# Four x tiles loaded ahead of the context's weights and split before them, and the second batch's matrix split in four parts

## The chip, the cores and the metric

The kernel runs on one core of one Trainium2 chip. The metric is the device time of one execution in microseconds (us), lower is better. Engine names are those of the profile: PE is TensorE's matmul side (PEld its weight loads), DVE is VectorE, ACT is ScalarE, POOL is GpSimd, SP is SyncE, which only issues transfers here.

## What is computed

Two batches of 2048 rows of 512 values pass through one decoder layer in f32: a self attention without softmax, a cross attention over 154 context rows with a mask, and a feed-forward step with a time shift, each followed by a layer norm.

```
attn = jnp.einsum('bhik,bhjk->bhij', q, k)          # self attention: no softmax, 8 heads of 64
out = jnp.einsum('bhik,bhkj->bhij', attn, v)        # so (q k^T) v = q (k^T v)
x = _layernorm(x + out @ w_o.T + b_o)
...
scores = jnp.einsum('bhqd,bhkd->bhqk', q, k) / jnp.sqrt(jnp.float32(D_K))   # 16 heads of 32, 154 keys
scores = jnp.where(Mask == 0, jnp.float32(NEG_INF), scores)
x = _layernorm(x + (softmax(scores) @ v) @ W_o.T + b_o)
...
xr = mu_r * x + (1.0 - mu_r) * x_prev ; xk = mu_k * x + (1.0 - mu_k) * x_prev
r = sigmoid(xr @ W_r.T) ; k_act = square(relu(xk @ W_k.T))
x = _layernorm(x + r * (k_act @ W_v.T))
```

Since the self attention has no softmax, it is one 512x512 matrix per batch, made from the sum of x^T x over the batch's rows. Each product that must keep f32's accuracy is made in three passes: both operands are split into a high part (a rounded copy, by ACT) and a low part (the difference, by DVE or POOL), and three of the four products are summed.

## The kernel before

There are two blocks with a barrier between them, each with one program written out by hand per engine. An engine runs its own list strictly in order; semaphores tie the lists together.

**The first block** (`prologue`) reads x in 32 tiles of 128 rows, 16 to a batch, through a ring of four buffers (`RING`). For tile j, SP loads it (`load(j)`, L183) once tile j-4 has been split and added; ACT makes the high part and its half (`high(j)`, L214 and L215); DVE adds the tile to a running column sum (L296) and makes the low part (`low(j)`, L300); PE adds the tile's products to four accumulator banks (`sums(j)`, L438 and L443). From tile 4 on `high(j)` waits until PE is done with tile j-4. Between these tiles stand the context's values and keys: ctx (616 KB), the value weights `cross_wv` and the key weights `cross_wk` (1 MB each) are loaded by SP, split by `part_high(i)` on ACT (L239) and `part_low(i)` on DVE (L330), i being 0 for ctx, 1 for cross_wv and 2 for cross_wk. PE multiplies them (three row tiles of values, then four column tiles of keys, L87 to L89), DVE takes the values with their bias (`v_raw`, L342), and ACT takes the keys (`kt`, L255). PE's list in the first block begins: tiles 0 to 5, values, keys, tiles 6 to 17. Later parts of the block fold the first batch's self attention into a matrix m.

**The second block** (`layers`) walks over 16 groups of 256 rows, 8 to a batch. Its lists are software-pipelined: in one turn with group n in the middle, group a = n + 1 starts (projection y, layer norm, queries, first scores), n goes through its softmax, f = n - 1 leaves the attention, and e = n - 2 goes through the feed-forward step. The second batch needs another matrix: SP loads it as `m_raw` during the turn in which a is 7 (the last group of batch 0), and it is split there, ACT writing `m_hi` (L855) and DVE `m_lo` (L1183). PE first reads them at the start of group 8 (`y_product`), which waits for `m_lo_ok`. What stands around the split in that turn:

- ACT: `take_q(7, 0)`, `k_high`, `mix_high`, m_hi, `take_q(7, 1)`, `o_high(6, 2)`, `take_turned(6, 3, 0)`, `exponentials(7, 0, 0)` (L744), `take_turned(6, 3, 1)` (L752), `take_rest(6, 3)` (L757)
- DVE: `k_mix_low`, `o_low(6, 2)` (L1016), m_lo, `masked_min(7, 0, 0)` and `masked_min(7, 0, 1)` (L1009), `v_finish(4, 0)`, then in the next turn `v_finish(4, 1)` and `o_low(6, 3)`
- PE: queries of 7, `values(6, 2)`, `scores(7, 0)`, transposes, the feed-forward's last product of group 4 (`v_product`, L87 to L89 on ffn_wv), `values(6, 3)` (L1464, L1468), which waits for `take_rest(6, 3)`, then in the next turn the first half of group 5's `k_product`, `scores(7, 1)`, `transposes(7, 0, 0)` and `o_product(6, 0)`, which waits for `o_low(6, 3)`

`exponentials(7, 0, t)` waits for `masked_min(7, 0, t)`, and POOL weighs their result (`weigh`, L1259 to L1265) before PE turns it. POOL's `add_bias` (L1276) also lies in this turn.

## Time and profile before

| | before |
|---|---|
| median of 3 runs | 939.41 us (938.14 to 939.75) |
| the profiled execution | 940.32 us |
| its span, first to last instruction | 938.2 us |
| mean granted TensorE clock | 0.994 |
| PE busy | 912.5 us, 97% of the span |
| DVE, ACT, POOL busy | 667.9, 552.4, 515.4 us |
| transfers | 34.10 MB read and 9.70 MB written, 47 GB/s over the span |

The profile is one execution. Between its span and its own time lie 2.1 us. Busy times of PE count a matmul to its modelled end, so what tells of PE are the stretches in which it waits and those in which its clock is at 0.5. In a timeline, columns are start (us), duration (us), engine, line, operation, output<-input, shapes and count; a bracket holds how long the engine was idle just before, and what ended it.

### The profile page before, as it was taken

What the parts mean: (1) busy time and instruction counts of PE and PEld (TensorE: products, weight loads), DVE (VectorE), ACT (ScalarE), POOL (GpSimd) and SP (SyncE); (2) the same over time, 40 slices, a digit from 0 to 9 for tenths busy, and PEclk for the clock granted to TensorE, in tenths of its full rate; (3) what the DMA queues carried; (4) which work ended last, traced back from release to release, by engine and by line L of the source; (5) the groups of instructions that cost most, each with busy time, mean ns of one, the idle gap of its engine ahead of it and who ended that gap; (6) DMA issues with size and microseconds to landing.
All of it is one profiled execution on the core that took longest, in us unless ns stands there. A gap on an engine that the chain in (4) does not pass through costs nothing.

```text
span 938.2 us, 18936 instructions
## 1 busy us (share of the span) xinstructions
PE 912.5 (97%) x6676; PEld 729.4 (78%) x6676; DVE 667.9 (71%) x1979; ACT 552.4 (59%) x1654; POOL 515.4 (55%) x507
## 2 busy tenths in 40 slices
PE   5999999998999999999999999999999999999997
PEld 5877657666788888887878787878787878787876
DVE  6487554556686877777777777777777777777775
ACT  6455305657675757575656575757575656666631
POOL 1034015657676666666566666675757584847421
PEclk9999999999999999999999999999999999999999
DMA  8593010102110101011100010010101010100001
GB/s 279 187 303 137 23 25 24 42 1 73 48 30 24 30 24 30 24 30 67 43 24 30 24 28 26 16 39 9 45 8 46 8 46 9 45 2 23 2 23 45
DMA packets 30872, 45.64 MB, mean 49 GB/s; under 512 B 2747, under 2 KB 15547, under 8 KB 30523
## 3 DMA queue, kind: packets, MB, share of 16 engines
q1 hardware_dynamic: 26123, 35.26, 11.7%
q10 hardware_dynamic: 4656, 9.18, 2.8%
q8 instruction: 54, 0.88, 0.4%
q14 instruction: 39, 0.32, 0.1%
HBM read 34.10 MB, written 9.70 MB: 47 GB/s over the span
## 4 chain that ended last, share of the span: by engine, by line
PE 77%; DVE 5%; issue 2%; ACT 2%; POOL 0%; POOLq 0%; DVEq 0%; ACTq 0%
PE dense L87 18%; PE dense L89 17%; PE dense L88 17%; PE turned L1450 6%; PE scores L1438 5%; PE rest_value L1464 4%; PE rest_value L1468 3%; PE dense L1350 2%; PE rest_value L1456 1%; PE turned L1350 1%; PE dense L1394 1%; PE scores L1356 1%; DVE mix_k_raw L1049 1%; DVE prob L1009 1%; ACT prob L744 1%
## 5 line engine op out<-in xcount | busy, mean ns | idle before, releaser
L1259 POOL TENSOR_TENSOR row_inv<-row_sum,minus_one 128x4 f32<-128x4 f32 x128 | 141.8, 1108 | 249.7 <-ACT prob L744 246.6
L744 ACT ACTIVATE prob<-prob,row_min 128x154 f32<-128x154 f32 x512 | 209.9, 418 | 16.8 <-DVE row_min L1009 16.8
L1265 POOL TENSOR_TENSOR prob<-prob,row_inv 128x512 f32<-128x512 f32 x128 | 147.0, 1148 | 0.0
L1009 DVE CUSTOM_DVE_ANT_0 prob<-scores,mask_add 128x154 f32<-128x154 f32 x512 | 129.3, 310 | 6.6 <-PE scores L1438 6.4
L752 ACT ACTIVATE prob_t<-turned 128x512 f32<-128x512 f32 x128 | 76.1, 595 | 61.8 <-PE turned L1450 60.5
L744 ACT ACTIVATION_READ_ACCUMULATOR prob<-prob,row_min 128x1 f32 x512 | 98.9, 193 | 0.0
L1016 DVE TENSOR_TENSOR o_t_lo<-rest_value,o_t_hi 128x256 fp32r<-128x256 f32 x64 | 26.9, 420 | 83.8 <-ACT o_t_hi L763 83.8
L1450 PE MATMUL turned<-ident,prob 128*128 128x128 f32 x512 | 79.4, 278 | 0.4 <-POOL prob L1265 0.4
L763 ACT ACTIVATE o_t_hi<-rest_value 128x256 fp32r<-128x256 f32 x64 | 24.5, 382 | 88.2 <-PE rest_value L1468 88.2
L87 PE MATMUL dense<-xt_hi,cross_wq_hi 128*128 128x256 f32 x256 | 74.2, 290 | 1.3 <-DVE xt_lo L1000 1.3
L87 PE MATMUL dense<-mix_k_hi,ffn_wk_hi 128*128 128x256 f32 x256 | 75.2, 294 | 0.0
L88 PE MATMUL dense<-mix_k_lo,ffn_wk_hi 128*128 128x256 f32 x256 | 72.5, 283 | 0.0
L89 PE MATMUL dense<-mix_k_hi,ffn_wk_lo 128*128 128x256 f32 x256 | 72.5, 283 | 0.0
L88 PE MATMUL dense<-xt_lo,cross_wq_hi 128*128 128x256 f32 x256 | 72.3, 283 | 0.0
L89 PE MATMUL dense<-xt_hi,cross_wq_lo 128*128 128x256 f32 x256 | 72.3, 282 | 0.0
L1450 PEld LDWEIGHTS turned<-ident,prob 128*128 128x128 f32 x512 | 58.9, 140 | 16.2 <-issue 9.3
L1264 POOL TENSOR_TENSOR prob_rest<-prob,row_inv 128x104 f32<-128x104 f32 x128 | 51.0, 398 | 10.0
L1049 DVE SCALAR_TENSOR_TENSOR mix_k_raw<-diff,cols,x_t 128x256 f32<-128x256 f32 x64 | 54.1, 904 | 0.0
L1276 POOL TENSOR_TENSOR x<-x,cross_bo_row 128x1024 f32<-128x1024 f32 x16 | 52.1, 3258 | 3.2 <-PE dense L1350 3.2
L87 PEld LDWEIGHTS dense<-mix_k_hi,ffn_wk_hi 128*128 128x128 f32 x256 | 49.0, 191 | 6.2 <-issue 6.2
L87 PE MATMUL dense<-cross_wo_hi,o_t_hi 128*128 128x512 f32 x128 | 52.8, 413 | 0.7 <-DVE o_t_lo L1016 0.7
L87 PE MATMUL dense<-m_hi,xt_hi 128*128 128x512 f32 x128 | 51.6, 403 | 1.6 <-ACT u L716 1.3
(266 smaller groups left out, 2602.7 us busy)
## 6 DMA issues: line engine op xcount, KB each, us to landing
x_rows<-x_rows SPq DMA_DIRECT2D x32, 256.0 KB, 4.7
xt_raw<-x_cols SPq DMA_DIRECT2D x16, 512.0 KB, 3.7
out<-gate_then_y SPq DMA_DIRECT2D x15, 512.0 KB, 2.8
mask_in<-mask SPq DMA_DIRECT2D x16, 154.0 KB, 2.3
cross_wv<-cross_wv SPq DMA_DIRECT2D x1, 1024.0 KB, 9.1
cross_wk<-cross_wk SPq DMA_DIRECT2D x1, 1024.0 KB, 9.7
self_wv<-self_wv ACTq DMA_DIRECT2D x1, 1024.0 KB, 5.6
self_wk<-self_wk ACTq DMA_DIRECT2D x1, 1024.0 KB, 10.4
```

Of the source, the lines that this page charges most:

```text
L87: pe.matmul(out, sta[0], mov[0], start=first, stop=False, skip_group_check=True)
L88: pe.matmul(out, sta[0], mov[1], start=False, stop=False, skip_group_check=True)
L89: return pe.matmul(out, sta[1], mov[0], start=False, stop=last, skip_group_check=True)
L744: m = act.activation(keys, keys, ACT.Exp, bias=row_min[:, buf, t, h:h + 1], scale=-1.0, accum_out=row_sum[:, buf, t, h:h + 1])
L752: act.activation(pt[:, 0:HPG, t * P:(t + 1) * P], t_bank[:].rearrange("p (c n) -> p c n", c=HPG), ACT.Copy).then_inc(*t_out.up)
L1009: m = dve.tensor_tensor_reduce(prob[buf][:, t, h * CTX:(h + 1) * CTX], s_bank[:, h, t * CTX:(t + 1) * CTX], mask_add[n % 2][:, t, :], -SCA ...
L1049: m = dve.scalar_tensor_tensor(mixed[g][:, k, :], diff[:, k, :], col_sb[:, c0 + k:c0 + k + 1], x2t[:, k, 0:GT], ALU.mult, ALU.add)
L1259: pool.tensor_tensor(row_inv[:, buf, t, :], row_sum[:, buf, t, :], minus_one[:], ALU.pow).then_inc(*p_inv.up)
L1264: pool.tensor_tensor(after, keys[:, :, P:CTX], inv.broadcast_to([P, HPG, CTX - P]), ALU.mult)
L1265: pool.tensor_tensor(keys[:, :, 0:P], keys[:, :, 0:P], inv.broadcast_to([P, HPG, P]), ALU.mult).then_inc(*p_norm.up)
L1276: pool.tensor_tensor(rows[:], rows[:], bo_row[:].unsqueeze(1).broadcast_to([P, TPG, D]), ALU.add).then_inc(*x1_bo.up)
L1450: m = pe.transpose(t_bank[:, h * P:(h + 1) * P], prob[g % 2][:, t, h * CTX:h * CTX + P], ident[:])
```

## The change

In the first block SP issues the loads of tiles 4 to 7 right behind ctx, and `cross_wv` and `cross_wk` behind all four; before, cross_wv stood ahead of tiles 4 and 5, and cross_wk, a bias row and cols ahead of tiles 6 and 7. ACT and DVE split tile 4 before ctx, and tiles 5 to 7 before cross_wv; cross_wv and cross_wk follow each other. ACT further splits tiles 8 to 11 before it takes the keys (before: behind them), and DVE does tiles 8 and 9 before it takes the values. PE does eight tiles instead of six before the values.

In the second block the split of the second batch's matrix becomes four instructions on each engine, one per 128x512 part. On ACT they stand before `take_q(7, 0)`, before `mix_high(5, "k")`, before `take_q(7, 1)` and behind it. On DVE two stand behind `masked_min(7, 0, 1)` and two behind `v_finish(4, 0)`; `masked_min(7, 0, ...)` thus comes before all of them.

```diff
             sp.dma_start(ctx_t[:], wide("ctx_cols")).then_inc(*ctx_in.up)
+            for j in range(RING, 2 * RING):
+                load(j)
             sp.dma_start(w_v[:], wide("cross_wv")).then_inc(*wv_in.up)
-            load(RING)
-            load(RING + 1)
             sp.dma_start(w_k[:], wide("cross_wk")).then_inc(*wk_in.up)
...
-            high(0, 1, 2, 3)
+            high(0, 1, 2, 3, 4)
             part_high(0)
-            high(4)
+            high(5, 6, 7)
             part_high(1)
-            high(5)
             part_high(2)
-            high(6, 7)
...
+            high(8, 9, 10, 11)
             act.wait_ge(*cols_in.at(0))
             for m in range(KT):
...
-            high(*range(8, 14))
+            high(12, 13)
...
-            low(0, 1, 2, 3)
+            low(0, 1, 2, 3, 4)
             part_low(0)
-            low(4)
+            low(5, 6, 7)
             part_low(1)
-            low(5)
             part_low(2)
-            low(6, 7)
+            low(8, 9)
             dve.wait_ge(*bv_in.at(0))
...
-            low(*range(8, 18))
+            low(*range(10, 18))
...
-            sums(0, 1, 2, 3, 4, 5)
+            sums(*range(2 * RING))
             pe.wait_ge(*part_lo.at(0, 2))
...
-            sums(*range(6, HALF + 2))
+            sums(*range(2 * RING, HALF + 2))
...
+            def next_m_high(k):
+                act.wait_ge(*m_here.at(0))
+                act.activation(m_hi[:, k, :], m_raw[:, k, :], ACT.Copy).then_inc(*m_hi_ok.up)
...
+                if a == GPB - 1:
+                    next_m_high(0)
                 take_q(a, 0)
...
-                    act.wait_ge(*m_here.at(0))
-                    act.activation(m_hi[:], m_raw[:], ACT.Copy).then_inc(*m_hi_ok.up)
+                    next_m_high(2)
                 take_q(a, 1)
+                if a == GPB - 1:
+                    next_m_high(3)
...
+            def next_m_low(*parts):
+                for k in parts:
+                    dve.wait_ge(*m_hi_ok.at(0, k + 1))
+                    dve.tensor_tensor(m_lo[:, k, :], m_raw[:, k, :], f32(m_hi[:, k, :]), ALU.subtract).then_inc(*m_lo_ok.up)
...
-                if a == GPB - 1:
-                    dve.wait_ge(*m_hi_ok.at(0))
-                    dve.tensor_tensor(m_lo[:], m_raw[:], f32(m_hi[:]), ALU.subtract).then_inc(*m_lo_ok.up)
                 masked_min(a, 0, 0)
                 masked_min(a, 0, 1)
                 if n == 1:
                     add_one()
+                if a == GPB - 1:
+                    next_m_low(0, 1)
                 if live(e):
                     v_finish(e, 0)
+                if a == GPB - 1:
+                    next_m_low(2, 3)
```

SP's list at the start of the first block, the loads behind ctx. The four ring buffers are named x_rows_79, 81, 83 and 85; the first of them holds tiles 0, 4, 8.

```order
 L187 DMA ctx_t<-ctx_cols 128x4x308
-L188 DMA cross_wv<-cross_wv 128x4x512
 L183 DMA x_rows_79<-x_rows 128x512
 L183 DMA x_rows_81<-x_rows 128x512
+L183 DMA x_rows_83<-x_rows 128x512
+L183 DMA x_rows_85<-x_rows 128x512
+L190 DMA cross_wv<-cross_wv 128x4x512
 L191 DMA cross_wk<-cross_wk 128x4x512
 L192 DMA bv_row<-rows 128x512
 L193 DMA cols<-cols 128x24
-L183 DMA x_rows_83<-x_rows 128x512
-L183 DMA x_rows_85<-x_rows 128x512
```

cross_wv now stands behind tiles 4 to 7, and cross_wk behind tiles 6 and 7 too.

DVE's list in the same place, from ctx's low part on, before:

```order
8 L330 TENSOR_TENSOR ctx_t_lo<-ctx_t,ctx_t_hi 128x1232
9 L296 TENSOR_TENSOR x_sum<-x_sum,x_rows_79 128x512
10 L300 TENSOR_TENSOR x_rows_lo<-x_rows_79,x_rows_both 128x512
11 L330 TENSOR_TENSOR cross_wv_lo<-cross_wv,cross_wv_hi 128x2048
12 L296 TENSOR_TENSOR x_sum<-x_sum,x_rows_81 128x512
13 L300 TENSOR_TENSOR x_rows_lo<-x_rows_81,x_rows_both 128x512
14 L330 TENSOR_TENSOR cross_wk_lo<-cross_wk,cross_wk_hi 128x2048
```

and now:

```order
8 L295 TENSOR_TENSOR x_sum<-x_sum,x_rows_79 128x512
9 L299 TENSOR_TENSOR x_rows_lo<-x_rows_79,x_rows_both 128x512
10 L329 TENSOR_TENSOR ctx_t_lo<-ctx_t,ctx_t_hi 128x1232
11 L295 TENSOR_TENSOR x_sum<-x_sum,x_rows_81 128x512
12 L299 TENSOR_TENSOR x_rows_lo<-x_rows_81,x_rows_both 128x512
13 L295 TENSOR_TENSOR x_sum<-x_sum,x_rows_83 128x512
14 L299 TENSOR_TENSOR x_rows_lo<-x_rows_83,x_rows_both 128x512
15 L295 TENSOR_TENSOR x_sum<-x_sum,x_rows_85 128x512
16 L299 TENSOR_TENSOR x_rows_lo<-x_rows_85,x_rows_both 128x512
17 L329 TENSOR_TENSOR cross_wv_lo<-cross_wv,cross_wv_hi 128x2048
18 L329 TENSOR_TENSOR cross_wk_lo<-cross_wk,cross_wk_hi 128x2048
```

Tile 5 no longer stands behind cross_wv's low part, and nothing stands between the two weights.

DVE's list around the split of m in the turn with a = 7, before (the ISA rows are `masked_min(7, 0, 0)`):

```order
798 L1055 TENSOR_TENSOR mix_k_lo<-mix_k_raw,mix_k_hi 128x1024
799 L1016 TENSOR_TENSOR o_t_lo<-rest_value,o_t_hi 128x256
800 L1183 TENSOR_TENSOR m_lo<-m_raw,m_hi 128x2048
801 L1009 ISA prob_90,row_min<-scores,mask_add_1356 128x154
802 L1009 ISA row_min 128x1
```

and now, from the last row of `masked_min(7, 0, 1)` to `o_low(6, 3)`:

```order
815 L1021 ISA row_min 128x1
816 L976 TENSOR_TENSOR m_lo<-m_raw,m_hi 128x512 x2
817 L1085 SCALAR_TENSOR_TENSOR gate_then_y<-gate_then_y,dense 128x512
818 L1088 SCALAR_TENSOR_TENSOR gate_then_y<-gate_then_y,x_0_97 128x512
819 L984 BN_STATS stats_1365<-gate_then_y 128x6
820 L986 BN_AGGR moments_1366<-stats_1365 128x2
821 L976 TENSOR_TENSOR m_lo<-m_raw,m_hi 128x512 x2
822 L1085 SCALAR_TENSOR_TENSOR gate_then_y<-gate_then_y,dense 128x512
...
827 L1028 TENSOR_TENSOR o_t_lo<-rest_value,o_t_hi 128x256
```

The whole low part stood ahead of the row minima of group 7; now its halves stand behind them, on either side of `v_finish(4, 0)`.

## Rows read from the trace of the kernel before

**Rows 1.** The page's busy times: busy us, share of the span, instructions.

```profile
PE 912.5 (97%) x6676; PEld 729.4 (78%) x6676; DVE 667.9 (71%) x1979; ACT 552.4 (59%) x1654; POOL 515.4 (55%) x507
```

**Rows 2.** PE's waits, whole execution: us in total, times, longest.

```profile
PE scores L438 <- DVE x_rows_lo L300: 9.4, 3, 4.9
PE rest_value L1464 <- ACT prob_t L757: 4.3, 3, 1.9
```

**Rows 3.** Busy times by stretch; behind POOL stands the granted TensorE clock.

```profile
13.00:19.30 6.30, 1.89 (x10) 1.34 (x9) 4.67 (x6) 6.30 (x8) 0.00 (x0) 1.00 0.74 270
19.30:22.70 3.40, 3.33 (x10) 2.89 (x11) 3.40 (x5) 1.41 (x3) 0.00 (x0) 0.50 0.82 289
...
473.00:477.00 4.00, 4.00 (x23) 4.00 (x22) 2.69 (x5) 1.36 (x4) 3.92 (x5) 0.57 0.01 4
```

**Rows 4.** PE's timeline, 9 to 38 us: tiles 2 to 6, the values' first product.

```profile
9.92 0.39 PE L438 MATMUL scores<-x_rows_lo,x_rows_both 128*128 128x512 f32 x1
...
11.43 0.39 PE L438 MATMUL scores<-x_rows_lo,x_rows_both 128*128 128x512 f32 x1
...
14.25 0.50 PE L438 MATMUL scores<-x_rows_lo,x_rows_both 128*128 128x512 f32 x1 [1.14 <-DVE x_rows_lo L300]
...
19.38 0.80 PE L438 MATMUL scores<-x_rows_lo,x_rows_both 128*128 128x512 f32 x1 [3.35 <-DVE x_rows_lo L300]
...
22.32 0.56 PE L87 MATMUL turned<-cross_wv_hi,ctx_t_hi 128*128 128x512 f32 x1
...
37.68 0.39 PE L438 MATMUL scores<-x_rows_lo,x_rows_both 128*128 128x512 f32 x1
```

**Rows 5.** DVE's timeline, 7 to 18 us.

```profile
7.82 0.68 DVE L300 TENSOR_TENSOR x_rows_lo<-x_rows,x_rows_both 128x512 fp32r<-128x512 f32 x1
...
10.04 1.44 DVE L330 TENSOR_TENSOR ctx_t_lo<-ctx_t,ctx_t_hi 128x1232 fp32r<-128x1232 f32 x1 [1.54 <-ACT ctx_t_hi L239]
...
15.82 2.29 DVE L330 TENSOR_TENSOR cross_wv_lo<-cross_wv,cross_wv_hi 128x2048 fp32r<-128x2048 f32 x1 [1.63 <-ACT cross_wv_hi L239]
```

**Rows 6.** ACT's timeline, 8 to 16 us.

```profile
8.77 1.23 ACT L239 ACTIVATE ctx_t_hi<-ctx_t 128x1232 fp32r<-128x1232 f32 x1 [0.73 <-DMA ctx_t<-ctx_cols]
...
13.90 1.90 ACT L239 ACTIVATE cross_wv_hi<-cross_wv 128x2048 fp32r<-128x2048 f32 x1
```

**Rows 7.** Transfers: us from issue to landing; tile 4 was issued at 4.92.

```profile
x_rows<-x_rows SPq DMA_DIRECT2D x1, 256.0 KB, 7.9
...
cross_wv<-cross_wv SPq DMA_DIRECT2D x1, 1024.0 KB, 9.1
cross_wk<-cross_wk SPq DMA_DIRECT2D x1, 1024.0 KB, 9.7
```

**Rows 8.** GB/s in 40 slices of 0 to 20 us, so 0.5 us each.

```profile
GB/s 0 0 0 106 172 381 352 250 250 284 273 268 282 338 302 260 306 291 389 414 401 401 410 406 401 389 385 385 387 380 370 379 386 328 258 107 33 0 33 123
```

**Rows 9.** ACT's timeline, turn with a = 7.

```profile
461.78 1.90 ACT L855 ACTIVATE m_hi<-m_raw 128x2048 fp32r<-128x2048 f32 x1
...
469.04 0.42 ACT L744 ACTIVATE prob<-prob,row_min 128x154 f32<-128x154 f32 x1 [3.87 <-DVE row_min L1009]
```

**Rows 10.** DVE's timeline, the same turn and the next one's start.

```profile
465.05 3.00 DVE L1183 TENSOR_TENSOR m_lo<-m_raw,m_hi 128x2048 fp32r<-128x2048 f32 x1
467.97 0.30 DVE L1009 CUSTOM_DVE_ANT_0 prob<-scores,mask_add 128x154 f32<-128x154 f32 x1
...
475.38 0.41 DVE L1016 TENSOR_TENSOR o_t_lo<-rest_value,o_t_hi 128x256 fp32r<-128x256 f32 x1
```

**Rows 11.** POOL's timeline, the same turn.

```profile
462.51 3.39 POOL L1276 TENSOR_TENSOR x<-x,cross_bo_row 128x1024 f32<-128x1024 f32 x1
```

**Rows 12.** PE's timeline, 469 to 479 us.

```profile
469.39 0.40 PE L89 MATMUL dense<-ffn_wv_hi,k_act_lo 128*128 128x512 f32 x1
471.67 0.64 PE L1464 MATMUL rest_value<-prob_t,v_rest 128*32 128x256 f32 x8 [1.88 <-ACT prob_t L757]
...
478.36 0.47 PE L87 MATMUL dense<-cross_wo_hi,o_t_hi 128*128 128x512 f32 x1
```

More of the change, by code:

```diff
@@ L193, in sp_program @@
             sp.dma_start(col_sb[:], io["cols"]).then_inc(*cols_in.up)
-            for j in range(RING + 2, 5 * RING):
+            for j in range(2 * RING, 5 * RING):
                 load(j)
@@ L629, in layers @@
         m_here, c_here = flag("m_here", 1, 16), flag("c_here", 1, 16)
-        m_hi_ok, m_lo_ok = flag("m_hi"), flag("m_lo")
+        m_hi_ok, m_lo_ok = flag("m_hi", KT), flag("m_lo", KT)
         x_here, x_hi_ok, x_lo_ok = flag("x_here", 1, 16), flag("x_hi_ok"), flag("x_lo_ok")
@@ L850, in act_program @@
                     k_high(e, 1)
+                if a == GPB - 1:
+                    next_m_high(1)
                 if live(f):
@@ L1187, in dve_program @@
                     add_one()
+                if a == GPB - 1:
+                    next_m_low(0, 1)
                 if live(e):
                     v_finish(e, 0)
+                if a == GPB - 1:
+                    next_m_low(2, 3)
             v_finish(LAST - 3, 1)
```

## The prediction

> **What bounds the kernel now.** I read the busy times first. PE is busy 97% of the span and no other engine above 71% [rows 1], so only what PE waits for, or what it does at half clock, can be won. Then PE's waits over the whole execution [rows 2]: 9.4 us for the low parts of x tiles, three times, and 4.3 us for the transposed probabilities in front of `values`, three times, the longest 1.9. Then where they lie. PE's timeline of the first block [rows 4] has gaps of 1.14 us before tile 4 and 3.35 us before tile 5; the rest of the 9.4 is the start, which no edit touches. The busy times by stretch [rows 3] add the clock: it stands at 1.00 over 13 to 19.3 us, where PE is busy 1.89 of 6.3 us, and at 0.50 (1.2 instead of 2.4 GHz) over the 3.4 us behind. The third place is 469 to 472 us, where `values(6, 3)` waits 1.88 us for ACT [rows 12], and the clock over 473 to 477 is 0.57 on average [rows 3]. From 22.7 us to the end of the first block PE waits for nothing but one 0.3 us, so what is won early stays won as long as the rest moves with it.
>
> **First block: the two gaps, at most 6.2 us.** 1.14 + 3.35 = 4.5 us of waiting, and 3.4 us at half clock are 1.7 us of lost work: 6.2 us. Each gap has its cause in a queue. Tile 4 was issued at 4.92 us and landed 7.9 us later, at 12.8 [rows 7], behind ctx and the 1 MB of cross_wv. Tile 5's low part stood on DVE behind cross_wv's (15.82 to 18.1 [rows 5]), which waited for ACT's cross_wv_hi, 13.90 to 15.8 [rows 6].
>
> What is late next? I rebuild the landings from the rate [rows 8]; summed up, it gives 2.06 MB by 9.0 us, then about 0.4 MB per us. Before, tile 4 was complete in the queue at 2.99 MB (tiles 0 to 3 1.05, ctx 0.63, cross_wv 1.05, itself 0.26), which the sum passes at 11.3 us, and it landed at 12.8: a lag of 1.5 us. The same way now: tile 4 ends at 1.94 MB, passed at 8.6, landing 10.1; tiles 5, 6, 7 at 10.9, 11.5 and 12.2; cross_wv at 3.78 MB, 13.3, landing 14.8; cross_wk 17.6. The queue doesn't run dry: tile 7 is issued when `low(3)` ends, 7.82 + 0.68 = 8.5 us [rows 5], cross_wv at about 9, when 0.67 MB still wait.
>
> Now the chains, with a tile at about 1.05 us on ACT and 1.2 on DVE, ctx at 1.2 and 1.4, a weight at 1.9 and 2.3 [rows 5, 6]. ACT: tile 4 10.1 to 11.1, ctx to 12.3, tiles 5 to 7 to 15.5, cross_wv 15.5 to 17.3. DVE: tile 4 to 11.4, ctx 12.4 to 13.8, tiles 5, 6, 7 to 15.0, 16.2, 17.4, cross_wv 17.4 to 19.7. PE needs 1.51 us per tile (9.92 to 11.43 [rows 4]) and is done with tile 3 at 13.0: tile 4 at once to 14.5, tile 5 waits 0.5 us for DVE, tiles 5 to 7 to 19.5, the values' products at 19.7. Two new waits, 0.7 us in all, too short by the rows to bring the clock down: behind the 1.14 us gap it stayed at 1.00 [rows 3]. So 6.2 - 0.7 = 5.5 us. Counter-check by position: the products began at 22.32, with six tiles done, now at 19.7 with eight, 22.32 - 19.7 + 2 x 1.51 = 5.6, and their first two ran at half clock. I take 5.6.
>
> The other edits of this block cost nothing while their cover stands. cross_wk_lo is ready at about 22, the keys' products begin 8.3 us behind the values', at 28. Tiles 8 to 11 take ACT some 4.2 us from about 20, while the first key tile can't be copied before 29.7: without that cover it would be those 4.2 us, for the key copies alone. ACT's own four loads move from 18.3 to about 19.5, and are first needed some 30 us later. PE does tile 8 at 37.68 + 3.0 - 5.6 = 35.1 us, with tiles 8 to 11 split long before; `high(12)` waits for tile 8's products, 36.6, and its low part is there at about 38, tile 12's turn is at 41.1.
>
> **Second block: the split of m, 3.4 us.** The chain of the 1.88 us wait goes DVE, ACT, PE: DVE's m_lo takes 465.05 to 468.0 [rows 10] ahead of the row minima of group 7, `exponentials(7, 0, 0)` starts at 469.04 after 3.87 us of idling [rows 9], and behind it stand on ACT the two copies that `values(6, 3)` needs, at 471.67 [rows 12]. Now the minima come first, at about 464.9, so the exponentials start near 466.1 (1.1 us behind, as before), the copies end near 468.7, and PE is free at 469.39 + 0.3 = 469.7: no wait, 1.9 us won. On ACT four parts of about 0.6 (0.52 apart, as half a tile) are 2.1 to 2.5 us against 1.90 [rows 9], but the last query copy stands behind three of them, and `o_high(6, 2)` comes out within 0.2 us of where it was. With the wait goes what I take to be its effect, the half clock behind it: (1 - 0.57) x 4 = 1.7 us [rows 3]. Together 3.6 us.
>
> Late next: `o_low(6, 3)`, at 475.38 on DVE [rows 10], for `o_product(6, 0)`, which comes at 478.36 - 3.6 = 474.8. DVE does eight minima to 466.8, two parts to 468.0, `v_finish(4, 0)` to 470.3, two parts to 471.5, `v_finish(4, 1)` to 474.1 or 474.7, `o_low` to 474.5 or 475.1. So a wait of 0 to 0.3 us; I take 0.2, and 3.4 us as the sum.
>
> m_lo took 3.00 us where the same shape took 2.29 in the first block [rows 5, 10]; it began at 465.05 while POOL's bias addition ran until 462.51 + 3.39 = 465.9 [rows 11]. Now the first parts come behind that, and the last two beside POOL's weighing. The Trainium skill (SBUF — State Buffer, Who interferes with whom) has a DVE instruction with two SBUF inputs and a GpSimd one that reads SBUF block each other in full; the 0.7 us of these rows, of 0.85 beside each other, agree. By it the last two parts could wait out the weighing's longest instruction, about 1 us, or hold it up by as much; the sum above has none of it.
>
> **Sum.** 5.6 + 3.4 = 9.0 us. From the profiled execution's 940.32 (938.2 of span and 2.1 around it) 931.3; it lies 0.9 above the median of 939.41, so the median after is 930.4.
>
> **Rivals.** (1) cross_wv becomes the bound. If it needs its 9.1 us from issue to landing again [rows 7], from 9.0, it lands at 18.1, is split by 22.3, and PE stands from 19.5 to 22.4. That gains 22.32 - 22.4 + 3.0 = 3.0, and if the clock falls behind the 2.9 us, 1.2. With 3.4 this gives 933.0 to 934.8. For it: three more tiles' worth of splitting and 0.5 MB stand ahead. Against: those 9.1 us were mostly queueing, and cross_wk's 9.7 with 3 MB issued before it too.
> (2) The second block gives part back: DVE or POOL is held up by the port, or the half clock stays, having another cause. 1.0 to 1.9 us of the 3.4 go: 931.4 to 932.3. For it: DVE has no slack before `o_low(6, 3)`. Against: the clock fell 1.6 us behind the wait and nowhere else between 22.7 us and the end.
> (3) The first block's gain is lost again, the change not doing in the end what it says: weights and x tiles issued later in the block come as before while PE is 5.6 us early. Leaves 3.4 us: 936.0. Against: those loads are issued by engines that move with PE.
> (4) Slower: DVE's tiles 8 and 9 now stand before the values' copies, and PE's second key product waits for the first of these. PE comes there at about 29.7 us. Tile 9, issued at about 15, is expected near 20; from a landing at 27.5 on every us counts fully, and from about 36.5 the kernel is slower than before, at 40 us 943. The longest landing in these rows is 9.7 us, which would be 25.
>
> **How the numbers follow.** Forecast 0.65, (1) 0.14, (2) 0.12, (3) 0.05, (4) 0.03, and 0.01 for no change at all. The forecast's own width is that of its bounds: 6.2 and 3.6 at best give 929.6, and the runs' scatter of 0.7 us goes below that, 928.9. Upward the range takes in (2) and (1) to 934.8. A measurement of this kernel can tell about 0.2%, 1.9 us, from no change. Cases (1) to (3) are all faster by more; I keep something back for (3) and (4) being worse than priced: faster 0.94, within 0.02, slower 0.04.
>
> **What would show it.** Right: PE gaps below 0.6 us before tiles 4 and 5 and before the values' first product, that product at about 19.7 us, clock 1.00 from 9 us on, tile 8 at 35, the first block 5.6 us shorter; no wait at the last `values` of the turn with a = 7, clock 1.00 there. Wrong: a gap of over 1 us before the values with cross_wv landing after 16 us (1), a half-clock stretch at 465 us without a wait (2), new waits of PE between 35 and 115 us (3), or in the keys' products (4).

## The result, and the profile after

| | before | after |
|---|---|---|
| median of 4 runs each, us | 939.19 (938.14 to 939.75) | 933.13 (932.96 to 933.36) |
| profiled execution, us | 940.32 | 933.12 |
| its span, us | 938.2 | 931.2 |
| mean granted TensorE clock in it | 0.994 | 0.998 |

The ratio of the medians is 0.9937, with a 95% interval of 0.992 to 0.9954. The changed kernel is 6.06 us faster by the medians and 7.07 us by the two spans. The forecast was 930.4 with 9.0 us of gain. Sign and range were right; the size was forecast half as large again as it came.

The page of the changed kernel gives the same picture as [rows 1], PE first and far ahead (busy us, share of the span, instructions).

```profile
PE 909.6 (98%) x6676; PEld 726.8 (78%) x6676; DVE 670.0 (72%) x1982; ACT 553.7 (59%) x1657; POOL 515.8 (55%) x507
```

PE's waits of the whole execution, in us in total, times, and the longest. They answer to [rows 2].

```profile
PE scores L436 <- DVE x_rows_lo L299: 4.9, 1, 4.9
PE rest_value L1477 <- ACT prob_t L759: 2.4, 2, 1.6
PE turned L87 <- DVE cross_wv_lo L329: 1.6, 1, 1.6
...
PE dense L87 <- DVE o_t_lo L1028: 1.3, 2, 0.7
```

Of the 9.4 us for low parts of x tiles the 4.9 us of the start are left, so both gaps of the first block are gone. Of the waits for `prob_t` the one of 1.9 us is gone. Two are new: 1.6 us before the values' products in the first block, and one of 0.60 us before `o_product(6, 0)` in the second (one of the two on the last line).

The mean clock counts more than what PE feels: in each of the thirteen profiled executions the clock also stands at half over the last 1.3 to 4.3 us, when PE has done its last matmul and nothing is lost by it. The 0.998 of after is this end alone.

PE's timeline shows the places (start and duration in us, engine, line, operation, tiles, in brackets the idle time before it and what ended it). They answer to [rows 4] and [rows 12].

```profile
20.82 0.50 PE L87 MATMUL turned<-cross_wv_hi,ctx_t_hi 128*128 128x512 f32 x1 [1.58 <-DVE cross_wv_lo L329]
...
36.07 0.39 PE L436 MATMUL scores<-x_rows_lo,x_rows_both 128*128 128x512 f32 x1
...
456.52 0.64 PE L1477 MATMUL rest_value<-prob_t,v_rest 128*32 128x256 f32 x8
...
465.22 0.64 PE L1477 MATMUL rest_value<-prob_t,v_rest 128*32 128x256 f32 x8
...
471.26 0.50 PE L87 MATMUL dense<-cross_wo_hi,o_t_hi 128*128 128x512 f32 x1 [0.60 <-DVE o_t_lo L1028]
```

To see where the 7.07 us come from I cut both executions at three points that both have: tile 8 on PE, the first of the eight-matmul steps of `values(6, 2)`, and the end. Before, tile 6 came at 37.68 [rows 4] and tile 8 3.03 us later, at 40.71; `values(6, 2)` started here, on PE's timeline of before:

```profile
461.14 0.64 PE L1464 MATMUL rest_value<-prob_t,v_rest 128*32 128x256 f32 x8
```

| stretch | before, us | after, us | gained |
|---|---|---|---|
| start to tile 8 | 40.71 | 36.07 | 4.64 |
| tile 8 to `values(6, 2)` | 420.43 | 420.45 | 0.0 |
| `values(6, 2)` to the end | 477.10 | 474.65 | 2.45 |

So nothing is lost in the 420 us between. Both terms of the sum came out smaller than forecast in these two executions, 4.6 for 5.6 and 2.45 for 3.4. The clock is at 1.00 in both places where it had fallen. Behind the 1.58 us wait, and where `values(6, 3)` had waited (columns: window, us, then busy us and count of PE, its weight loads, DVE, ACT and POOL, the granted clock, DMA share, GB/s; [rows 3] has the same of before):

```profile
19.00:22.70 3.70, 2.12 (x10) 1.58 (x9) 3.35 (x2) 2.67 (x3) 0.00 (x0) 1.00 0.99 344
...
466.00:470.00 4.00, 4.00 (x49) 3.49 (x41) 3.86 (x8) 2.51 (x7) 3.92 (x5) 1.00 0.02 6
```

### The profile page after: what moved, and what is told of

Same layout as the page of the kernel before. It is cut to its first block, busy times and chain, and to the rows that moved or that the text cites. A ratio compares the mean times of both kernels' runs of the same rounds, so it can differ in the third digit from the quotient of the medians.

```text
span 931.2 us, 18942 instructions
## 1 busy us (share of the span) xinstructions
PE 909.6 (98%) x6676; PEld 726.8 (78%) x6676; DVE 670.0 (72%) x1982; ACT 553.7 (59%) x1657; POOL 515.8 (55%) x507
## 4 chain that ended last, share of the span: by engine, by line
PE 77%; DVE 6%; issue 2%; ACT 1%; POOL 0%; POOLq 0%; DVEq 0%; ACTq 0%
PE dense L87 18%; PE dense L89 17%; PE dense L88 17%; PE turned L1463 6%; PE scores L1451 5%; PE rest_value L1477 4%; PE rest_value L1481 3%; PE dense L1363 2%; PE rest_value L1469 1%; PE turned L1363 1%; PE dense L1407 1%; PE scores L1369 1%; DVE mix_k_raw L1061 1%; DVE prob L1021 1%; DVE stats L984 1%
```

## The experiments

All kernels of this section compute the whole output. Times are medians, and each stands beside a median of the kernel before that was measured together with it: 939.23 for e1 to e4, 938.91 for e5 to e7, 938.3 for e8 to e11. "Start" means the start of the values' first product, "tail" the time from `values(6, 2)` to the end.

### The two halves apart

e1 is the kernel before with the changed orders of the first block alone.

```diff
-            high(0, 1, 2, 3)
+            high(0, 1, 2, 3, 4)
             part_high(0)
-            high(4)
+            high(5, 6, 7)
             part_high(1)
...
-            sums(0, 1, 2, 3, 4, 5)
+            sums(*range(2 * RING))
```

> The first block as changed, the second as before. If the two halves of the change add up, the first tile behind the keys starts on PE 4.6 us earlier in step (as in the changed kernel), the 1.88 us wait of the last values product in the turn with a = 7 and the half-clock stretch behind it are still there, and the span is about 933.6 us, 4.6 below before. The rival, that part of the first block's gain is lost again in later loads, would show as new PE waits before 120 us and a span above 934.5.

e2 is the kernel before with the split of m alone.

```diff
+                if a == GPB - 1:
+                    next_m_high(0)
                 take_q(a, 0)
...
                 if a == GPB - 1:
-                    act.wait_ge(*m_here.at(0))
-                    act.activation(m_hi[:], m_raw[:], ACT.Copy).then_inc(*m_hi_ok.up)
+                    next_m_high(2)
...
-                if a == GPB - 1:
-                    dve.wait_ge(*m_hi_ok.at(0))
-                    dve.tensor_tensor(m_lo[:], m_raw[:], f32(m_hi[:]), ALU.subtract).then_inc(*m_lo_ok.up)
```

> The first block as before, the second as changed. Adding up: a span of 935.7 to 935.8 us, 2.45 below before, with gaps of 1.1 and 3.4 us before tiles 4 and 5, no wait at the last values product of the turn with a = 7, clock 1.00 behind it, and a 0.6 us wait of o_product for o_low(6, 3). If the half clock there has another cause than the wait, it stays and the span is about 937.4.

Measured: e1 934.48, ratio 0.9954 (0.9939 to 0.9969), e2 937.55, ratio 0.9979 (0.9968 to 0.999). In medians -4.75 and -1.7, together 6.4, where the whole change has 6.06: they add up within their intervals. The old first block is not the same in each execution either: in e2 the gap before tile 4 was 0.28 us instead of 1.14, the one before tile 5 3.36. The surprise is in e1's trace, at a step whose order e1 leaves as it was; e1's expectation had a half-clock stretch there, and a span of 933.6 us, where 932.0 came. PE's timeline, and the stretches behind it:

```profile
466.90 0.64 PE L1462 MATMUL rest_value<-prob_t,v_rest 128*32 128x256 f32 x8 [1.88 <-ACT prob_t L755]
```

```profile
468.00:471.00 3.00, 3.00 (x28) 2.86 (x28) 2.86 (x6) 1.60 (x4) 2.92 (x4) 1.00 0.02 5
471.00:474.00 3.00, 3.00 (x29) 2.53 (x29) 2.14 (x11) 2.21 (x6) 3.00 (x3) 1.00 0.01 3
```

The wait is the 1.88 us of [rows 12] to the hundredth, and the clock stays at 1.00 behind it, where [rows 3] has 0.57. The tail is 475.59 against 477.10 of before, with the same instructions in the same order. So 1.5 us of the tail's 2.45 us between the two profiled executions is the clock, and it is not there in every execution. The order by itself gives 475.59 - 474.65 = 0.94 us. The tail repeats well where the clock doesn't fall: 474.60 to 474.68 in the six profiled executions with the changed second block and no fall behind `values(6, 2)` (after, e2, and e5, e6, e7 and e11 below).

### The second block: what gives half of it back

Four variants of the split, all with the changed first block. e3 has ACT's and DVE's part whole, and only moves `m_lo` behind the row minima (the diff of this step is against the kernel before, those of the other three against the changed kernel).

```diff
                     o_low(n, 2)
+                masked_min(a, 0, 0)
+                masked_min(a, 0, 1)
                 if a == GPB - 1:
                     dve.wait_ge(*m_hi_ok.at(0))
                     dve.tensor_tensor(m_lo[:], m_raw[:], f32(m_hi[:]), ALU.subtract).then_inc(*m_lo_ok.up)
-                masked_min(a, 0, 0)
-                masked_min(a, 0, 1)
```

> First block as changed. In the second, m's two parts stay one instruction each, ACT's at its old place; DVE's stands behind masked_min(7, 0, 1). If the gain comes from the order alone and not from cutting in four, the wait of the last values product is gone here too (at most 0.3 us left) and the span is within 0.4 us of the changed kernel's 931.2. If the cutting matters, ACT's 1.9 us copy ahead of the queries keeps 1 us or more of the wait and the span is 932.2 or more.

e4 is the changed kernel with DVE's second pair of parts one turn later, behind `o_low(6, 3)`.

```diff
+                if a == GPB:
+                    next_m_low(2, 3)
...
-                if a == GPB - 1:
-                    next_m_low(2, 3)
```

> The changed kernel with the last two parts of m's low part moved behind o_low(6, 3) on DVE. If the 0.6 us wait of o_product(6, 0), and the 0.85 us that PE loses between its scores and that product, come from the 1.4 us that these two parts take in front of v_finish(4, 1), both go: a span of about 930.5. If v_finish(4, 1) is late because its products end late, nothing moves, and if the two parts then hold up the next row minima, the loss comes back at a later wait: 931.2.

e9 keeps DVE's pairs and makes ACT's part whole again; e10 keeps ACT's four parts and makes DVE's part whole behind the minima.

```diff
-                if a == GPB - 1:
-                    next_m_high(0)
                 take_q(a, 0)
...
-                    next_m_high(2)
+                    act.wait_ge(*m_here.at(0))
+                    act.activation(m_hi[:], m_raw[:], ACT.Copy).then_inc(*m_hi_ok.up)
```

> The changed kernel with ACT's high part of m as one instruction at its old place, DVE's low part in pairs as changed. Theory: cutting ACT's copy puts a 0.5 us part ahead of mix_high(5, k), DVE's mix_k_lo thereby starts behind POOL's bias addition instead of ahead of it and takes 3.42 instead of 1.73 us beside it, and o_low(6, 3) is late by that. Then mix_k_lo takes 1.7 us here, the 0.6 us wait for o_low is gone, and from the start of the values product of (6, 2) to the end 473.6 us pass, as in e3, instead of 474.65. Rival: the low part in two pairs around v_finish is what makes o_low late; then 474.4 or more.

```diff
-                    next_m_low(0, 1)
+                    dve.wait_ge(*m_hi_ok.at(0))
+                    dve.tensor_tensor(m_lo[:], m_raw[:], f32(m_hi[:]), ALU.subtract).then_inc(*m_lo_ok.up)
...
-                if a == GPB - 1:
-                    next_m_low(2, 3)
```

> The changed kernel with DVE's low part of m as one instruction behind masked_min(7, 0, 1), ACT's high part in four as changed: the other half of the same test. Theory: mix_k_lo still takes about 3.4 us, o_low is late, and from the start of the values product of (6, 2) to the end 474.6 us pass. Rival (the pairs make o_low late): mix_k_lo's length doesn't matter and 473.6 us pass.

| | ACT's m_hi | DVE's m_lo | time, us | tail, us | wait of `o_product(6, 0)` |
|---|---|---|---|---|---|
| after | four parts | two pairs | 933.13 | 474.65 | 0.60 |
| e10 | four parts | whole | 933.06 (one run) | 474.48 | 0.20 |
| e9 | whole | two pairs | 932.38 (one run) | 473.61 | none |
| e3 | whole | whole | 931.71, ratio 0.9925 (0.9908 to 0.9942) | 473.63 | none |
| e4 | four parts | two pairs, one late | 933.94, ratio 0.9948 (0.9932 to 0.9964) | 475.30 | none |

The tail follows ACT's column. With ACT's part whole it is 473.6 (also in e8, below), with four parts it is 0.85 to 1.0 us longer, however DVE cuts its part. The last column names less than is lost: counted from `values(6, 2)`, `o_product(6, 0)` starts after 13.73 us in e9, 14.53 in e10 and 14.74 in after, and the rest of the loss lies in stops too short to be listed. The tails are compared here because tile 8 alone differs by more than that between executions (below), and the times contain both. e3's span was 929.4 us, below both values that its expectation named: it gained 1.0 us on the changed kernel in the tail and 0.75 in the first block.

DVE's and POOL's timelines show how an ACT edit gets to `o_low`. First e9 (DVE, then POOL), then after (DVE, then POOL):

```profile
456.48 0.68 DVE L1074 TENSOR_TENSOR k_act_lo<-square,k_act_hi 128x512 fp32r<-128x512 f32 x1
457.42 1.73 DVE L1062 TENSOR_TENSOR mix_k_lo<-mix_k_raw,mix_k_hi 128x1024 fp32r<-128x1024 f32 x1 [0.26 <-ACT mix_k_hi L795]
...
460.56 0.31 DVE L1016 CUSTOM_DVE_ANT_0 prob<-scores,mask_add 128x154 f32<-128x154 f32 x1
```

```profile
456.48 1.58 POOL L1273 TENSOR_TENSOR prob<-prob,row_inv 128x512 f32<-128x512 f32 x1
458.03 3.40 POOL L1284 TENSOR_TENSOR x<-x,cross_bo_row 128x1024 f32<-128x1024 f32 x1
```

```profile
456.37 1.56 DVE L1079 TENSOR_TENSOR k_act_lo<-square,k_act_hi 128x512 fp32r<-128x512 f32 x1
457.85 3.42 DVE L1067 TENSOR_TENSOR mix_k_lo<-mix_k_raw,mix_k_hi 128x1024 fp32r<-128x1024 f32 x1
461.20 0.41 DVE L1028 TENSOR_TENSOR o_t_lo<-rest_value,o_t_hi 128x256 fp32r<-128x256 f32 x1
461.53 0.30 DVE L1021 CUSTOM_DVE_ANT_0 prob<-scores,mask_add 128x154 f32<-128x154 f32 x1
```

```profile
456.35 1.04 POOL L1278 TENSOR_TENSOR prob<-prob,row_inv 128x512 f32<-128x512 f32 x1
457.34 2.85 POOL L1289 TENSOR_TENSOR x<-x,cross_bo_row 128x1024 f32<-128x1024 f32 x1
```

In e9 `k_act_lo` and POOL's weighing of the probabilities start in the same hundredth, and POOL is the one that takes longer: 1.58 us, against 1.04. In the changed kernel the first quarter of m_hi stands ahead of `k_act_hi` on ACT (454.47, so `k_act_hi` ends at 456.34), DVE starts 0.02 us behind POOL, and now DVE takes longer: 1.56 instead of 0.68. From there POOL is ahead: its bias addition starts 0.5 us before `mix_k_lo`, and `mix_k_lo` takes 3.42 us instead of 1.73. The two DVE instructions end 457.93 - 457.39 = 0.54 and 461.27 - 460.19 = 1.08 us behind POOL's. That is about what the work of their 512 and 1024 columns takes, since the 2048 columns of m_lo in e3 took 2.28 us. So DVE stood still while POOL's instruction ran. The Trainium skill (SBUF — State Buffer, Who interferes with whom) has this as "Issue order, not op shape, decides who blocks", and these rows agree on who stands still. On POOL's side they show less than a full stop: in e9 the bias addition begins 1.1 us before `mix_k_lo` ends and takes 0.55 us more than in the changed kernel. That the first of ACT's four parts is the one that does it is read from these timelines; no run moves it alone.

Counted from `values(6, 2)`, the row minima (the last DVE line of each) start 6.83 us behind it in before and e1, 3.90 in e9, 3.91 in e3 and 5.01 in the changed kernel (461.53 - 456.52). So the cut of ACT's part gives 1.1 of the 2.9 us back, and `o_low(6, 3)`, three more steps down DVE's queue, comes 14.26 us behind `values(6, 2)` instead of 13.16 (e9), which is the new wait.

e4 asks whether the wait can be avoided by clearing DVE before `o_low` instead. It does avoid it: `o_product(6, 0)` doesn't wait. But the late pair then runs beside POOL's 2.44 us `xt_lo` (470.42), and what stands behind the pair is late, so that the y products wait. DVE, then PE:

```profile
469.92 3.49 DVE L976 TENSOR_TENSOR m_lo<-m_raw,m_hi 128x512 fp32r<-128x512 f32 x2
```

```profile
478.17 0.47 PE L87 MATMUL dense<-m_hi,xt_hi 128*128 128x512 f32 x1 [1.06 <-DVE x L1034]
```

The wait of 0.60 became one of 1.06 us further down. Its tail is 0.65 us longer than that of the changed kernel. Its span of 931.8 us, where the expectation named 930.5 and 931.2, holds another 1.2 us between tile 8 and `values(6, 2)`, from a clock that fell at another place (last section).

### The first block: when cross_wv lands

The forecast had the values' first product at 19.7 us, the changed kernel has it at 20.82. ACT's and DVE's timelines show why.

```profile
8.74 0.63 ACT L214 ACTIVATE x_rows_both<-x_rows 128x512 fp32r<-128x512 f32 x1 [0.85 <-DMA x_rows<-x_rows]
...
16.52 1.92 ACT L239 ACTIVATE cross_wv_hi<-cross_wv 128x2048 fp32r<-128x2048 f32 x1 [2.11 <-DMA cross_wv<-cross_wv]
```

```profile
18.47 2.29 DVE L329 TENSOR_TENSOR cross_wv_lo<-cross_wv,cross_wv_hi 128x2048 fp32r<-128x2048 f32 x1 [2.38 <-ACT cross_wv_hi L239]
```

Tile 4 came at 8.74 us, 1.4 before its estimate, and cross_wv at 16.5, 1.7 after its own. ACT stands idle for 2.11 us for it, and PE starts 4.3 us behind the landing (1.9 of ACT, 2.3 of DVE and the steps between). Three experiments move cross_wv in the queue. e5 and e6 issue it behind tile 6 and tile 5, without touching the orders on ACT, DVE and PE; e7 issues cross_wk ahead of it.

```diff
-            for j in range(RING, 2 * RING):
+            for j in range(RING, 7):
                 load(j)
             sp.dma_start(w_v[:], wide("cross_wv")).then_inc(*wv_in.up)
+            for j in range(7, 2 * RING):
+                load(j)
```

> The changed kernel with cross_wv's load issued behind tile 6's, tile 7's behind it. Theory: cross_wv lands at 16.5 us because it is issued only at 8.9, behind the wait for low(3), and the queue has little to move from 9.5 to 11.5 us. Then it is issued at about 7.7 here, lands near 15.3, and the values' products wait 0.4 us instead of 1.58: a span of about 930.0. Rival: the landing is set by the bytes ahead and their rate; then 0.26 MB less ahead brings it 0.7 us, but tile 7 comes 2.6 us later and DVE's order makes cross_wv_lo no earlier: 931.0 or more.

```diff
-            for j in range(RING, 2 * RING):
+            for j in range(RING, 6):
                 load(j)
             sp.dma_start(w_v[:], wide("cross_wv")).then_inc(*wv_in.up)
+            for j in range(6, 2 * RING):
+                load(j)
```

> The changed kernel with cross_wv's load issued behind tile 5's, tiles 6 and 7 behind it. By the theory of the late issue cross_wv is issued at about 6.5 us and lands near 14; tiles 6 and 7 land behind it at about 14.5 to 15, so that tile 6 is late by 1 us or so but the values' products begin at about 19.8 without a wait of their own for the weights: a span of 930.0 to 930.6. By the rival (bytes and rate) tiles 6 and 7 land 2.6 us later than now and PE waits for them as it did for tile 5 before: 931.5 or more.

```diff
-            sp.dma_start(w_v[:], wide("cross_wv")).then_inc(*wv_in.up)
             sp.dma_start(w_k[:], wide("cross_wk")).then_inc(*wk_in.up)
+            sp.dma_start(w_v[:], wide("cross_wv")).then_inc(*wv_in.up)
```

> The changed kernel with cross_wk loaded ahead of cross_wv (the splits in their old order). cross_wv lands 2.6 us later, at about 19, so the values' products wait 4.2 us instead of 1.58: 2.6 us more, and if a wait of over 3 us brings the clock to half behind it, as behind tile 5's gap before, 1.7 us on top. Spans: 933.8 without and 935.5 with the fall of the clock. If something else than cross_wv's landing holds the products, less than 1 us is lost.

Measured: e5 933.65, ratio 0.9938 (0.9916 to 0.996); e6 934.09, ratio 0.9936 (0.9913 to 0.996); e7 937.82, ratio 0.9984 (0.9971 to 0.9996).

e5 and e6 give nothing. ACT's timeline of e5, then of e6:

```profile
16.21 0.64 ACT L216 ACTIVATE x_rows_both<-x_rows 128x512 fp32r<-128x512 f32 x1 [2.88 <-DMA x_rows<-x_rows]
...
17.27 1.90 ACT L241 ACTIVATE cross_wv_hi<-cross_wv 128x2048 fp32r<-128x2048 f32 x1
```

```profile
15.71 0.63 ACT L216 ACTIVATE x_rows_both<-x_rows 128x512 fp32r<-128x512 f32 x1 [2.58 <-DMA x_rows<-x_rows]
...
17.81 1.90 ACT L241 ACTIVATE cross_wv_hi<-cross_wv 128x2048 fp32r<-128x2048 f32 x1
```

The first tile behind cross_wv lands at about 16 us, and it stands ahead of cross_wv in ACT's order. The split starts 0.7 to 1.3 us later than in the changed kernel. ACT waits for the queue either way. cross_wv itself had landed by then: issued at 7.66 it took 7.8 us (15.5) in e5, issued at 6.48 it took 8.5 us (15.0) in e6. Their expectations had it at 15.3 and 14, and both spans (932.0 and 932.4) came on the side of the rival.

e7 does the reverse, and prices a late cross_wv. It lands at 19.4 (issued 9.21, 10.2 us under way), 2.9 later than in the changed kernel. PE's timeline and the stretch with its granted clock:

```profile
23.70 0.73 PE L87 MATMUL turned<-cross_wv_hi,ctx_t_hi 128*128 128x512 f32 x1 [4.09 <-DVE cross_wv_lo L329]
```

```profile
22.60:26.10 3.50, 2.40 (x6) 1.94 (x7) 3.50 (x3) 3.50 (x7) 0.00 (x0) 0.67 0.92 344
```

The start is 2.9 us later, and tile 8 4.5 us later (40.56 against 36.07). The rest, 1.6 us, is the half clock behind the 4.09 us wait. This is the first rival of the prediction with its clock, and a harder case of it: a wait of 4.09 us where the rival had 2.9, and 0.15 us of the first block's gain left (40.56 against 40.71) where it had 1.2. What is left in all, 1.1 us of medians, is near e2's 1.7.

### cross_wv in halves, and the changed kernel again

If the wait is the landing plus 4.3 us of splitting, it goes when PE starts on the first half of cross_wv. e8 is e3 with `cross_wv` split in two halves on ACT and DVE, the second half awaited before the third contraction step.

```diff
-                act.activation(to_split[i][1][:], to_split[i][0][:], ACT.Copy).then_inc(*part_hi.up)
+                for ks in ((slice(0, 2), slice(2, 4)) if i == 1 else (slice(0, 4),)):
+                    act.activation(to_split[i][1][:, ks, :], to_split[i][0][:, ks, :], ACT.Copy).then_inc(*part_hi.up)
...
+                    if r == 0 and k == 2:
+                        pe.wait_ge(*part_lo.at(0, 3))
```

> The kernel of e3_m_low_whole_behind_minima with cross_wv split in two halves on ACT and DVE, PE starting the values' products on the first half. If their wait is the chain landing, 1.9 us on ACT, 2.3 us on DVE, then they can start 2.2 instead of 4.3 us behind the landing, so behind any landing from 15.3 to 16.5 us they start right behind tile 7, at about 19.6 us, and tile 8 at about 34.9; with e3's second block the span is 929.0 (354 us... that is, 4.6 to 5.8 us of the first block and 3.5 of the second below before's 938.2, whatever the landing). If the half clock or a later queue sets the end, the span stays at e3's 929.4 or above although the wait is gone.

> The changed kernel itself once more, for the scatter of its first block. If the time from cross_wv's issue to its landing varies between executions of the same program (6.4, 6.7, 7.4 and 7.6 us so far with one and the same first block), the values' products start anywhere from 19.7 to 20.8 us here, and the timed runs spread over about 1 us or more around 933; if 7.6 us belongs to this program, they start at 20.8 again.

Measured together: e8 930.45 (929.95 to 932.22), ratio 0.9928 (0.9913 to 0.9944); the changed kernel again 932.9 (931.29 to 933.01), ratio 0.9948 (0.9933 to 0.9962). ACT, DVE and PE of e8:

```profile
16.64 2.01 ACT L240 ACTIVATE cross_wv_hi<-cross_wv 128x1024 fp32r<-128x1024 f32 x2 [1.91 <-DMA cross_wv<-cross_wv]
```

```profile
17.73 2.36 DVE L331 TENSOR_TENSOR cross_wv_lo<-cross_wv,cross_wv_hi 128x1024 fp32r<-128x1024 f32 x2 [1.32 <-ACT cross_wv_hi L240]
```

```profile
19.39 0.40 PE L87 MATMUL turned<-cross_wv_hi,ctx_t_hi 128*128 128x512 f32 x1
```

The landing is as late as in the changed kernel, 16.6, and PE doesn't wait. Tile 8 comes at 34.54, the tail is 473.62, and both terms of the forecast are there in size, with 1.5 us of the second owed to the clock in the profile of before. In the three executions of the changed first block with such a landing (after, e9, e10: 16.4 to 16.7) tile 8 comes at 36.0 to 36.2, 1.5 us later. e8 had the lowest median, but the times don't rank it: its interval and that of the changed kernel overlap by 0.1%, and e3, which lacks the halves, has a ratio of 0.9925 to its 0.9928. It is the traces that show the step by which it is faster.

The changed kernel's second profile differs from its first in the first block only. ACT's timeline:

```profile
14.69 1.92 ACT L239 ACTIVATE cross_wv_hi<-cross_wv 128x2048 fp32r<-128x2048 f32 x1 [0.39 <-DMA cross_wv<-cross_wv]
```

cross_wv landed at 14.7, where the estimate had 14.8, PE started on the values at 18.99, and tile 8 came at 34.30, 1.8 us before that of the first profile. Nothing in the program differs. The first block is the same in seven profiled executions (both of the changed kernel, e1, e3, e4, e9, e10): cross_wv took 5.8 to 7.6 us from issue to landing, and tile 8 came between 34.30 and 36.24 us, with 35.91 in the middle. In the five in which PE is seen to wait for it (the first of the changed kernel, e1, e3, e9, e10), in e11 and in e7 the values' first product starts 4.29 to 4.30 us behind the landing.

## Why the prediction came out as it did, point by point

**The bound and the two places: right.** What PE waited for and the clock behind it were the whole gain between the two profiles. Both gaps before tiles 4 and 5 and the 1.88 us wait are gone, and the clock is 1.00 in both places. Between the two blocks nothing moved (420.43 and 420.45 us), so the third rival, a gain lost in between, is out. So is the fourth: from 20.82 us, the values' first product, to tile 8 PE's timeline has no wait.

**The first block: the mechanism right, the term mis-sized, 5.6 forecast and 4.64 measured**, and 4.5 to 6.4 over the seven profiles. The step that failed is cross_wv's landing at 14.8 us, rebuilt from two figures of before as if they were properties of the queue: about 0.4 MB per us [rows 8], and 1.5 us from a load's last byte in the sum to its landing. It came at 16.5. Before, cross_wv's megabyte was queued from 3.06 us on. Now the last of tiles 4 to 7, with cross_wv behind it, is issued only when `low(3)` has freed a buffer, at about 8.5 and 8.87 us. The stretch of 9.5 to 11.5 us, first of before, then of after (columns as above):

```profile
9.50:11.50 2.00, 2.00 (x14) 1.78 (x13) 1.44 (x1) 0.51 (x1) 0.00 (x0) 1.00 1.05 407
```

```profile
9.50:11.50 2.00, 2.00 (x14) 1.76 (x13) 1.05 (x2) 2.00 (x4) 0.00 (x0) 1.00 0.80 176
```

The rate there goes with how early a megabyte is queued: 407 GB/s in before (3.06), then e6 (6.48) and e5 (7.66), one execution each:

```profile
9.50:11.50 2.00, 2.00 (x13) 1.75 (x12) 1.36 (x2) 1.69 (x3) 0.00 (x0) 1.00 0.99 346
```

```profile
9.50:11.50 2.00, 2.00 (x13) 1.75 (x12) 1.05 (x3) 2.00 (x4) 0.00 (x0) 1.00 0.85 278
```

It is 176 to 244 in all nine that issue the first one at 8.7 or later. "The queue doesn't run dry" is only part of it: the DMA engines were busy for 0.80 instead of 1.05 and yet moved less than half, so what they moved also went more slowly. At 176 instead of 407 GB/s 0.46 MB less are moved in these two us. Summed as in the prediction, the 3.78 MB up to cross_wv's end are reached at 14.4 us instead of 13.3, 1.1 of the 1.7 us; the rest is the lag to the landing, 2.1 instead of 1.5 us. The second profile of the changed kernel (231 GB/s there) reaches the same sum at 13.9 and lands 0.8 us behind it, at 14.7. So between equal programs it is the lag that differs more, and the depth of the hole doesn't order the landings: e3 has 177 GB/s and 15.7 us, e1 244 and 16.3. What sets the lag I can't tell from these runs.

That PE starts on the values 4.3 us behind the landing is shown by e7 (landing and start both 2.9 us later) and by e8, where halves take the wait away at the same landing. The first rival named the right engine and the right wait, and its sign of being wrong came true in the first profile (a gap of over 1 us, 1.58, with cross_wv landing after 16 us). Its price was too high: 1.58 us of waiting instead of 2.9, 1.0 us of the term instead of 2.6, and no fall of the clock, which only e7 had.

**The second block: 3.4 forecast, 2.45 measured, by two errors of different kinds.** The first is in the term "half clock behind it, 1.7 us". Between the two profiled executions it is there, 1.5 us. But e1 has the same wait without it, so it doesn't follow from the order each time: that the term nearly came true for these two executions is luck, and without the fall the change is worth 0.94 us here. The second is "the minima at about 464.9", 3.8 us behind `values(6, 2)`: e3 and e9 have them 3.9 behind it, the changed kernel 5.0. The prediction weighed POOL against m_lo only, and costed ACT's four parts at 0.2 us for `o_high(6, 2)`. The queue that they were moved past also holds `k_act_hi`, and the 0.5 us there turned the order of two starts on DVE and POOL. That is the second rival's mechanism (the port, 1.0 of 3.4 us), at another instruction than I named. The late-next step, `o_low(6, 3)` with a wait of 0 to 0.3 us, was the right place: it is 0.60 with the 1.1 us and none without. In the terms of the sum the order was put at 1.9 - 0.2 = 1.7 us and measured 0.94.

**The offset to the median: wrong by 0.9.** The profiled execution of before lay 1.1 us above the median now measured, 939.19, and that of after on its own. The prediction carried 0.9 over as if it belonged to the profiler. Beside the experiments the kernel before ran 41 times more, from 935.84 to 941.49 us. Its five executions with a mean clock of 0.999 took 935.84 to 936.79, the five with 0.992 took 940.25 to 941.08. So the offset is mostly a clock that fell more in one execution than in another. The changed kernel's nine executions, at 0.998 or 0.999, took 931.29 to 933.36.

This bears on the first block's term too. The profile of before has two stretches of 3.4 us at half clock; one of them alone takes 0.0018 off the mean, and the end of the execution at least 0.0007 more, so a mean of 0.999 leaves no room for a stretch of this length. By it the clock fell in those five executions neither behind the gap before tile 5 nor behind the later wait, and they average 936.4 us. By this estimate the order is worth about 3.6 us against the 932.8 that the nine of the changed kernel average, and the other 2.4 us of the 6.06 are a clock that fell in 36 of the 41 executions of the one and, as far as its mean tells, in none of the nine of the other. How long the gaps were in the five, no trace shows. The prediction had put the clock at its full price in two places, 1.7 + 1.7 us.

Of the 2.7 us between 930.4 and 933.13, 0.96 are the first block's term, 0.95 the second's and 0.9 the offset; 0.1 goes the other way, around the span.

## What to carry to other kernels

A term for a clock that fell behind a wait should be taken from several executions, or be given a chance instead of a full price; the same holds for the landing of a load at the start, which here scatters by almost 2 us. Compare the executions with the highest mean clock of either kernel too: they tell what the order is worth by itself. Where a large load is gated by buffers that come free late, don't carry the old rate over, and split the load so that the engine behind it can start on its first part. Work that is cut into parts and spread over a queue delays each instruction in between, and where two engines get in each other's way, as DVE and POOL here, a few hundredths of a us at the start decide which of them stands still.

## What the runs showed of the hardware that I had not expected

**The same wait, with and without a fall of the clock.** 1.88 us of waiting at `values(6, 3)` had the clock at 0.57 of full speed behind it in before, that is for a part of the stretch at 1.2 GHz, and at 1.00 in e1 with the same instructions ahead. In e4 it fell elsewhere, behind waits of 0.83 us (to 162.03) and 0.95 us (to 164.05):

```profile
162.60:166.00 3.40, 2.45 (x32) 1.62 (x23) 1.91 (x6) 1.77 (x7) 3.06 (x5) 0.74 0.00 0
```

The changed kernel has the same two waits (0.83 at 163.22, 0.95 at 165.25), and the clock stands at 1.00 over 160 to 170 us. In the first block 1.58 us of waiting left it at 1.00 and 4.09 us (e7) did not. What makes it fall behind one of two equal waits these runs don't show.

**One load, 5.8 to 7.8 us.** The same 1 MB load, issued at 8.84 and 8.87 us by the same program, lands at 14.7 in one execution and at 16.5 in the other. Over the seven executions with this first block, and e8 with 7.8 us, it was issued between 8.82 and 9.06 us and landed between 14.7 and 16.7. This alone moves tile 8 by 1.9 us, about the 0.2% that the measurement of this kernel can tell from no change.
